# Reloads and the last matrix in quarter pieces: sixteen DMAs a chunk in place of four

## The chip, the cores and the metric

The kernel runs on one core of one Trainium2 chip, as one launch. The metric is the device time of that launch in microseconds (us). The engines are TensorE (PE), VectorE (DVE), ScalarE (ACT), GpSimd (POOL) and SyncE (SP). Each runs its own list of instructions in order; they meet only at semaphores. SyncE computes nothing here: it waits and issues DMAs, and 16 DMA engines carry out what SyncE, ScalarE and GpSimd issue.

## The reference

Two layers of a graph convolution on 6250 nodes and 200000 random edges, then a gather and a dense layer:

```python
def gcn_conv(x, W, b, src, dst, n):
    h = x @ W
    ...                                     # self loops, D^-1/2 (A+I) D^-1/2
    msgs = h[s] * norm[:, None]
    return jax.ops.segment_sum(msgs, d, num_segments=n) + b

g = jax.nn.relu(gcn_conv(service_emb, W1, b1, src, dst, 6250))
g = gcn_conv(g, W2, b2, src, dst, 6250)
ctx = g[context_idx].reshape(512, -1)                       # 3 x 32 features
x = jnp.concatenate([user_emb[user_idx], ctx], axis=1)      # 512 x 128
return x @ fc_W + fc_b                                      # 512 x 6250, float32
```

## The kernel before

**The adjacency as a matrix.** The kernel sorts the edges on VectorE (the first 310 us or so) and then builds the adjacency matrix in one-byte numbers from one-hot rows. Nodes lie in 49 blocks of 128. The matrix is built in chunks of destination blocks: `SIZES = [1, 2, 2] + [4] * 11`, that is `NG = 14` groups g. A group of 4 blocks has 196 tiles of 128 x 128 bytes, 25088 bytes in each of the 128 partitions. For each group, layer 1 is computed as soon as its tiles stand (`pair` and `aggregate` on TensorE, lines 1430 and 1448 into `psY`).

**Spill and reload.** SBUF holds three such groups in the slots of layer 1 (`SLOTS = 3`), and two more when the one-hot rows are no longer needed. The last three groups (11, 12, 13) stay; the other eleven are written to the DRAM tensor `adjacency_spill` (line 572) and read back for layer 2. `ORDER` is the order of layer 2: 11, 12, 13, 10, 9, ... 0. So places 3 to 10 of it are reloads of 4 blocks, 11 and 12 of 2 blocks, and 13 of 1 block. The prediction counts chunks by these places.

**Layer 2.** For place i, TensorE waits on `loaded` (line 1497) and on the PSUM tile of place i - 3, runs one matmul for each tile (`spread`, line 1448 into `pp`) and raises `y2_done`. VectorE reduces the tile (line 1220), finishes it (lines 1222 and 1212), and ScalarE's queue writes it to the DRAM table `context_table` (line 801), in rows of 128 bytes. SyncE runs ahead:

```python
sp.wait_ge(filled, pairs_before(NG))
for i in range(3, NG):
    if i >= 5:
        sp.wait_ge(y2_done, i - 4)
    part = -(-bytes_of(ORDER[i]) // LOAD_PARTS)
    for c in range(0, LOAD_PARTS * part, part):
        w = min(part, bytes_of(ORDER[i]) - c)
        sp.dma_start(...).then_inc(loaded[place2[i]], 16)        # line 597
for k in range(2):
    sp.wait_ge(y2_done, NG - 4 + k)
    load_fc(place2[(NG + k) % 5], k)
```

So the load for place i waits until place i - 5, whose slot it takes, is through; `load_fc` brings `fc_W` (k = 0, two DMAs a piece, since the rows of the user features are put behind the others, lines 584 and 585) and `fc_b` (k = 1, one row spread over all partitions, line 587). `fc_W` waits until place 9 is through, `fc_b` until place 10.

**The end.** GpSimd gathers three rows of the table for each of four batches (line 675), when the whole table is written. TensorE transposes the features (line 1529), multiplies them by W2 (line 1534), and then both TensorE (line 1538) and VectorE (line 1292) wait for all pieces of `fc_W` and `fc_b`. Then 4 x 13 matmuls in float32 (line 1549) are added to `fc_b` (line 1305) and written out by SyncE and ScalarE (line 522). Between layer 2 and the features TensorE runs 36 products of no use (`run_up`, line 1456).

Of the kernel before, what the change touches and what calls it, by code (L numbers as in the profile page):

```python
# [91 lines left out]
SPILL_PARTS = 4  # L92
RUN_UP = (8, 12, 36)
AHEAD_OF = {1: 12, 3: 6}
LOAD_PARTS = 4
FC_PART = 1568


UNIT = 2.0 ** -9
# [67 lines left out]
def bytes_of(g):  # L167
    return -(-tiles_of(g) // 2) * 2 * P
# [34 lines left out]
def gcn_kernel(nc, user_idx, context_idx, edge_index, user_emb, service_emb,  # L203
# [13 lines left out]
    with ctx:  # L217
# [309 lines left out]
        def _(sp):  # L527
# [50 lines left out]
            def load_fc(slot, what):  # L578
                tile = at(adj_at[slot], N * 4, F32)
                whole = fc_W if what == 0 else fc_b[None, :].to_broadcast((P, N))  # L580
                for c in range(0, N, FC_PART):
                    w = min(FC_PART, N - c)
                    if what == 0:
# [5 lines left out]
            with sp.If(is_bad == 0):  # L589
# [7 lines that stand above are left out]
# [220 lines left out]
        def _(dve):  # L817
# [468 lines left out]
            def mix_features(b):  # L1286

                dve.wait_ge(feat_mixed, b + 1)
                V.tensor_scalar(featT[0:CTX * D, b * P:(b + 1) * P], psX[0:CTX * D, b % 2 * P:(b % 2 + 1) * P], bias2[:, 0:1], None, ALU.add).then_inc(feat_ready, 1)  # L1289
            copy_features(0)  # L1290
            mix_features(0)
            dve.wait_ge(fc_in, 48 * -(-N // FC_PART))
            n = 0
# [15 lines left out]
        def _(pe):  # L1309
# [181 lines left out]
            with pe.If(is_bad == 0):  # L1491
                for i, g in enumerate(ORDER):
                    c = chunks_of(g)
                    tile = pp[i % 3]
                    if i >= 3:
                        pe.wait_ge(y2_read, i - 2)
                        pe.wait_ge(loaded[place2[i]], 16 * LOAD_PARTS * (i // 5 + (1 if i % 5 >= 3 else 0)))
                    for b in range(NH):
# [32 lines left out]
            def weigh_features(b):  # L1531

                pe.wait_ge(feat_copied, b + 1)
                MM(psX[0:CTX * D, b % 2 * P:(b % 2 + 1) * P], W2b[:], featT[0:CTX * D, b * P:(b + 1) * P], start=True, stop=True).then_inc(feat_mixed, 1)
            pe.wait_ge(users_in, 16 * BB)
            turn_features(0)
            weigh_features(0)
            pe.wait_ge(fc_in, 48 * -(-N // FC_PART))
            n = 0
# [33 lines left out]
```

## Time and profile before

| | us |
|---|---|
| three timed runs | 768.8, 770.29, 771.91 |
| their median | 770.29 |
| profiled execution | 772.33 |
| span of its instructions | 770.5 |
| TensorE busy | 587.4 (76%) |
| VectorE busy | 600.2 (78%) |
| ScalarE busy | 422.5 (55%) |
| GpSimd busy | 182.4 (24%) |
| TensorE's granted clock, mean | 0.92 of full speed |

All times are counted from the start of the span. "Busy" counts neither waits nor the issue of DMAs; the issues of SyncE's queue are rows of their own, marked SPq, whose length is the time that SyncE spent on them. "Issue" as the end of an idle time means that the engine waited for nothing that the profile shows. The share of the DMA engines is a mean over 16; it can come out a little over 1. The queues are q1 (SyncE), q10 (ScalarE), q0 (GpSimd), and q8 and q14, which carry instructions.

### The profile page before, as it was taken

How to read it: one execution, taken by the hardware profiler on the slowest of the kernel's cores; microseconds unless marked ns; L12 is line 12 of the kernel's file. 1: busy time of each engine (PE TensorE's matmuls, PEld its weight loads, DVE VectorE, ACT ScalarE, POOL GpSimd, SP SyncE). 2: the span in 40 equal slices, each digit the busy share in tenths (PEclk: the TensorE clock that was granted, in tenths of full speed). 3: DMA queues.
4: the chain of work that ended last, by engine and by line, in shares of the span. 5: the costliest groups of instructions: out<-in, count | busy, mean ns of one | idle time of the engine just before them, and what ended most of it. 6: DMA issues, size and time to landing. Idle time of an engine off the chain costs nothing.

```text
span 770.5 us, 21867 instructions
## 1 busy us (share of the span) xinstructions
PE 587.4 (76%) x9504; PEld 551.6 (72%) x9504; DVE 600.2 (78%) x1436; ACT 422.5 (55%) x770; POOL 182.4 (24%) x181
## 2 busy tenths in 40 slices
PE   0404662676929735478699999999999999997997
PEld 0304662675928725478699999999999998997643
DVE  9999999988999999787999999999984211111376
ACT  4993389797999111247588888888877000000000
POOL 1100000000000200377776666676200000000500
PEclk9999995978978965589899999999999999999999
DMA  7000000000000000235366665565200999859386
GB/s 127 2 0 1 1 1 1 1 2 1 2 3 2 5 0 1 58 92 173 100 211 209 209 209 205 183 204 199 66 3 3 359 414 408 289 153 303 86 316 284
DMA packets 39143, 94.13 MB, mean 122 GB/s; under 512 B 19097, under 2 KB 21843, under 8 KB 39044
## 3 DMA queue, kind: packets, MB, share of 16 engines
q1 hardware_dynamic: 24340, 74.28, 26.2%
q0 software_dynamic: 5216, 9.91, 6.1%
q10 hardware_dynamic: 9488, 8.52, 3.4%
q8 instruction: 76, 1.25, 0.7%
q14 instruction: 23, 0.19, 0.1%
HBM read 48.50 MB, written 44.18 MB: 120 GB/s over the span
## 4 chain that ended last, share of the span: by engine, by line
PE 55%; DVE 34%; issue 3%; ACT 3%; POOL 2%; DMA 1%; SPq 0%; DVEq 0%; POOLq 0%
PE pp L1430 17%; PE pp L1448 14%; PE psY L1448 13%; DVE arena L960 12%; DVE arena L961 11%; PE pp L1549 5%; PE psY L1346 3%; DVE arena L947 2%; POOL arena L655 2%; ACT arena L711 2%; PE pp L1366 1%; PE psX L1417 1%; DVE arena L958 1%; DVE arena L959 1%; DVE arena L955 1%
## 5 line engine op out<-in xcount | busy, mean ns | idle before, releaser
L1430 PE MATMUL pp<-arena 128*128 128x128 fp8e4 (+1 forms) x2401 | 189.4, 221 | 7.5 <-DVE arena L1140 6.3
L788 ACT ACTIVATE arena<-pp 128x512 uint16<-128x512 f32 x308 | 172.1, 584 | 42.0 <-PE pp L1430 39.7
L655 POOL DMA_INDIRECT arena<-ordered_keys,window x147 | 161.3, 1097 | 128.3 <-DMA ordered_keys<-arena 62.0
L711 ACT ACTIVATE arena<-arena,neg_word 128x780 fp8e4<-128x780 bf16 (+1 forms) x200 | 170.3, 942 | 10.4 <-PE psY L1346 10.4
L1430 PEld LDWEIGHTS pp<-arena 128*128 128x128 fp8e4 (+1 forms) x2401 | 148.4, 98 | 8.0 <-issue 6.0
L1448 PE MATMUL psY<-arena 128*128 128x96 bf16 x2401 | 150.5, 207 | 2.4 <-ACT y_s L772 2.1
L1448 PEld LDWEIGHTS psY<-arena 128*128 128x128 fp8e4 x2401 | 123.3, 98 | 2.9 <-ACT arena L788 2.6
L1139 DVE TENSOR_SCALAR arena<-arena 128x384 int32<-128x384 int32 (+5 forms) x224 | 110.8, 495 | 7.7 <-PE pp L1430 7.6
L1448 PE MATMUL pp<-arena 128*128 128x96 bf16 x2401 | 104.2, 206 | 9.0 <-issue 8.9
L1448 PEld LDWEIGHTS pp<-arena 128*128 128x128 fp8e4 x2401 | 102.7, 98 | 10.6 <-issue 10.5
L960 DVE TENSOR_TENSOR arena<-arena 128x832 f32<-128x832 f32 (+4 forms) x121 | 107.5, 889 | 3.1
L961 DVE TENSOR_TENSOR arena<-arena 128x832 f32<-128x832 f32 (+4 forms) x121 | 106.8, 883 | 0.0
L1366 PE MATMUL pp<-ident,arena 128*128 128x128 f32 x202 | 38.0, 361 | 77.1 <-DVE arena L961 75.8
L1346 PE MATMUL psY<-arena 128*128 128x128 fp8e4 x1024 | 69.2, 232 | 28.2 <-DVE arena L947 28.2
L1366 PEld LDWEIGHTS pp<-ident,arena 128*128 128x128 f32 x202 | 32.7, 189 | 80.3 <-DVE arena L961 78.5
L1346 PEld LDWEIGHTS psY<-arena 128*128 128x128 fp8e4 x1024 | 69.0, 141 | 29.1 <-issue 28.0
L1220 DVE TENSOR_REDUCE arena<-pp 128x128 f32<-128x384 f32 (+2 forms) x14 | 7.1, 507 | 94.4 <-PE pp L1448 94.4
L1140 DVE TENSOR_SCALAR arena<-arena 128x384 int32<-128x384 int32 (+5 forms) x224 | 72.7, 325 | 0.0
L764 ACT ACTIVATE arena<-arena,neg_low 128x128 f32<-128x128 f32 x147 | 47.9, 392 | 18.3 <-DMA arena<-ordered_keys,window 18.3
L640 POOL DMA_INDIRECT feat<-in_L_rec_user_emb_dram,ucl x4 | 4.6, 1146 | 218.1 <-DVEq L972 217.2
L675 POOL DMA_INDIRECT feat<-context_table,ccl x12 | 11.3, 945 | 173.5 <-DMA context_table<-arena 170.1
L1549 PE MATMUL pp<-arena 128*128 128x512 f32 (+1 forms) x104 | 43.1, 568 | 0.5 <-DVE arena L1289 0.5
(205 smaller groups left out, 543.6 us busy)
## 6 DMA issues: line engine op xcount, KB each, us to landing
arena<-adjacency_spill SPq DMA_DIRECT2D x32, 784.0 KB, 10.5
adjacency_spill<-arena SPq DMA_DIRECT2D x24, 768.0 KB
adjacency_spill<-arena SPq DMA_DIRECT2D x8, 832.0 KB
out_dram<-arena SPq DMA_DIRECT2D x12, 512.0 KB, 3.8
out_dram<-arena ACTq DMA_DIRECT2D x8, 512.0 KB, 3.8
arena<-adjacency_spill SPq DMA_DIRECT2D x8, 392.0 KB, 5.0
arena<-ordered_keys,window POOLq DMA_INDIRECT x147
arena<-in_L_rec_fc_b_dram SPq DMA_DIRECT2D x3, 784.0 KB, 12.1
```

The lines of the kernel that those rows point to most:

```text
L655: nc.gpsimd.indirect_dma_start(gath[:, k, q, :], None, ordered, bass.IndirectOffsetOnAxis(ap=window[:, q, d:d + 1], axis=0)).then_inc(gat[ ...
L711: ins = nc.scalar.activation(cols8[n % BUFS][:, 4 * u:4 * u + 4, 0:c1 - c0], high4[:, :, c0:c1], ACT.Sign, bias=neg_word[:, u:u + 1], satu ...
L788: nc.scalar.mul(adj16[g % SLOTS][:, m0 * P:m1 * P], bank(gp)[:, 0:(m1 - m0) * P], PAIR_SCALE).then_inc(evicted, 1)
L960: V.tensor_tensor(o_low, low, high, ALU.min)
L961: return V.tensor_tensor(o_high, low, high, ALU.max)
L1139: V.tensor_scalar(src32[h][:, i, :, 0:b - a], bit32[:, 0:4, a:b].bitcast(I32), abs(BIT - i), BITS, shift, ALU.bitwise_and)
L1140: ins = V.tensor_scalar(dst32[h][:, i, :, 0:b - a], bit32[:, 4:8, a:b].bitcast(I32), abs(BIT - i), BITS, shift, ALU.bitwise_and)
L1346: ins = MM(counts_of(s), cols8[n % BUFS][:, :, i], rows8[n % BUFS][:, :, i, :], start=False, stop=False)
L1366: ins = nc.tensor.transpose(ps[q][:, b * P:(b + 1) * P], src[:, c + b * P:c + (b + 1) * P], ident[:])
L1430: ins = MM(bank(gp)[:, (n - n0) // 2 * P:((n - n0) // 2 + 1) * P], src_hot(h, n - a), dst_hot(h, n - a), start=n % 2 == 0, stop=n % 2 == 1 ...
L1448: return MM(tile[:, dd * D3:(dd + 1) * D3], adj_tile(slot, n), features(layer, b), start=(n == 0), stop=(n == NH * c - 1))
L1549: MM(bank(n)[:, 0:w], featT[:, b * P:(b + 1) * P], fcW[:, c:c + w], start=True, stop=True).then_inc(fc_mm, 1)
```

## The change

Two constants change. Each reload is cut into sixteen pieces in place of four: 1568 bytes a partition where it was 6272 (for the groups of 2 blocks 784 where it was 3136, for the one of 1 block 400 where it was 1600). `fc_W` and `fc_b` go in pieces of 392 columns (1568 bytes) in place of 1568 columns. The counts in the waits follow. Nothing else changes; the lists of the other four engines are the same.

```diff
-LOAD_PARTS = 4
-FC_PART = 1568
+LOAD_PARTS = 16
+FC_PART = 392
```

SyncE's list before, from the branch behind the spills to the branch behind the loads of `fc_b` (`x32` stands for 32 of them in a row; `arena` is the SBUF area of all slots):

```order
L589 COMPARE_AND_BRANCH
L597 DMA arena<-adjacency_spill 128x6272 x32
L597 DMA arena<-adjacency_spill 128x3136 x8
L597 DMA arena<-adjacency_spill 128x1600 x4
L584 DMA arena<-in_L_rec_fc_W_dram 96x1568
L585 DMA arena<-in_L_rec_fc_W_dram 32x1568
```

Now the same place reads:

```order
L589 COMPARE_AND_BRANCH
L597 DMA arena<-adjacency_spill 128x1568 x128
L597 DMA arena<-adjacency_spill 128x784 x32
L597 DMA arena<-adjacency_spill 128x400 x16
L584 DMA arena<-in_L_rec_fc_W_dram 96x392
L585 DMA arena<-in_L_rec_fc_W_dram 32x392
```

There are 176 reloads where there were 44, and nothing has moved past them. Behind them, the pair of lines 584 and 585 came four times (the last with 1546 columns) and comes sixteen times (the last with 370). The end of the loads, in the list before:

```order
L584 DMA arena<-in_L_rec_fc_W_dram 96x1546
L585 DMA arena<-in_L_rec_fc_W_dram 32x1546
L587 DMA arena<-in_L_rec_fc_b_dram 128x1568 x3
L587 DMA arena<-in_L_rec_fc_b_dram 128x1546
L589 UNCONDITIONAL_BRANCH
```

and now:

```order
L584 DMA arena<-in_L_rec_fc_W_dram 96x370
L585 DMA arena<-in_L_rec_fc_W_dram 32x370
L587 DMA arena<-in_L_rec_fc_b_dram 128x392 x15
L587 DMA arena<-in_L_rec_fc_b_dram 128x370
L589 UNCONDITIONAL_BRANCH
```

The last piece of `fc_b`, for which the first matmul of line 1549 waits, is the 224th DMA of SyncE in this stretch; before it was the 56th.

## Rows read from the trace of the kernel before

**Rows 1.** The page: span, busy time by engine, chain by engine.

```profile
span 770.5 us, 21867 instructions
...
PE 587.4 (76%) x9504; PEld 551.6 (72%) x9504; DVE 600.2 (78%) x1436; ACT 422.5 (55%) x770; POOL 182.4 (24%) x181
...
PE 55%; DVE 34%; issue 3%; ACT 3%; POOL 2%; DMA 1%; SPq 0%; DVEq 0%; POOLq 0%
```

**Rows 2.** Groups by line, 598:714: count, busy, mean ns, idle before.

```profile
L1448 PE MATMUL pp<-arena 128*128 128x96 bf16 x2401 | 104.2, 206 | 9.0 <-issue 8.9
```

**Rows 3.** Timeline of TensorE: start, length, instructions, idle before.

```profile
612.86 5.60 PE L1448 MATMUL pp<-arena 128*128 128x96 bf16 x128 [0.23 <-issue]
...
672.91 27.55 PE L1448 MATMUL pp<-arena 128*128 128x96 bf16 x639 [0.82 <-issue]
701.81 5.57 PE L1448 MATMUL pp<-arena 128*128 128x96 bf16 x127 [1.35 <-issue]
710.02 2.67 PE L1448 MATMUL pp<-arena 128*128 128x96 bf16 x59 [2.63 <-issue]
```

**Rows 4.** DMA queues in 598:712, in 645.2:648, and in 626.5:628.5 (no instructions).

```profile
q8 instruction: 18, 0.29, 1.0%
...
q8 instruction: 1, 0.02, 2.1%
...
q1 hardware_dynamic: 146, 0.82, 97.5%
```

**Rows 5.** Timeline of VectorE: the reductions behind places 8 to 10.

```profile
681.40 0.56 DVE L1220 TENSOR_REDUCE arena<-pp 128x128 f32<-128x384 f32 x1 [8.34 <-PE pp L1448]
...
698.06 0.56 DVE L1220 TENSOR_REDUCE arena<-pp 128x128 f32<-128x384 f32 x1 [7.12 <-PE pp L1448]
```

**Rows 6.** The chain that ended last, 713 us on: start, length, what.

```profile
713.53 2.25 DMA context_table<-arena
...
723.22 7.11 PE pp L1549 x16
```

**Rows 7.** Timeline of SyncE's queue: start, length, DMAs issued.

```profile
598.29 4.13 SPq L597 DMA_DIRECT2D arena<-adjacency_spill  x8
...
626.59 1.74 SPq L597 DMA_DIRECT2D arena<-adjacency_spill  x4
...
645.26 2.62 SPq L597 DMA_DIRECT2D arena<-adjacency_spill  x4
...
663.45 2.37 SPq L597 DMA_DIRECT2D arena<-adjacency_spill  x4
...
690.04 1.58 SPq L585 DMA_DIRECT2D arena<-in_L_rec_fc_W_dram  x1
...
697.98 2.76 SPq L587 DMA_DIRECT2D arena<-in_L_rec_fc_b_dram  x4
...
L597 SPq DMA_DIRECT2D arena<-adjacency_spill x44: 319/432/1306, 598.3 to 682.6; - x44
```

**Rows 8.** DMA issues from 676 us: count, KB, median us from issue to landing.

```profile
arena<-adjacency_spill SPq DMA_DIRECT2D x4, 200.0 KB, 2.9
...
arena<-in_L_rec_fc_b_dram SPq DMA_DIRECT2D x1, 773.0 KB, 15.5
```

**Rows 9.** Queue q1 in 622:630, 672:678.5, 681.5:685.5; then engines in 683:683.5.

```profile
q1 hardware_dynamic: 574, 3.21, 96.6%
...
q1 hardware_dynamic: 578, 1.61, 71.5%
...
q1 hardware_dynamic: 539, 0.77, 65.1%
...
683.00:683.50 0.50, 0.50 (x16) 0.50 (x14) 0.00 (x0) 0.00 (x0) 0.00 (x0) 1.00 1.04 368
```

**Rows 10.** Stages by window (clock, DMA share, GB/s last); TensorE afterwards.

```profile
374.00:380.00 6.00, 3.65 (x39) 3.68 (x40) 5.86 (x19) 2.18 (x5) 4.59 (x5) 0.50 0.18 51
...
376.35 0.90 PE L1430 MATMUL pp<-arena 128*128 128x128 fp8e5 x7 [5.83 <-DVE arena L1140]
```

## The prediction

> **What bounds the kernel now.** I read the page first: the profiled span is 770.5 us (the execution itself 772.33 us; the median of the three timed runs is 770.29 us, so a difference in the span is carried over to the median as it is). No engine is full over the whole span and the chain is made mostly of TensorE and VectorE work [rows 1]. The change touches only DMAs that SyncE issues after the last aggregation of layer 1, so what counts is the stretch from 598 us to the end.
>
> In that stretch TensorE runs layer 2: fourteen chunks of matmuls of line 1448, each ended by the reduction of line 1220 on VectorE. The groups by line show 104.2 us of matmuls and 8.9 us in which TensorE stood still while it waited for nothing that the profile shows ("issue") [rows 2]. The timeline of TensorE shows their form: blocks of about 128 matmuls (5.60 us), and between them 0.2 to 0.8 us of idle time, then one of 1.35 and one of 2.63 us [rows 3]. From 672.91 us on, 639 matmuls run without a gap: there the DMA engines are no longer full. The gaps recur at a fixed number of instructions, and a 16 KB packet of the instruction queue is seen per block (18 from 598 to 712 us [rows 4]). I read them as fetches of TensorE's instructions that come late behind data packets. No wait on a reload shows anywhere: chunks without a gap follow each other at 8.33 us (from 681.40 to 698.06 us in two [rows 5]).
>
> Behind layer 2 the chain is: last reduction, the write of the table (2.25 us), three gathers on GpSimd, a transpose, and the first matmul of line 1549 at 723.22 us; from there TensorE sets the pace to the end, 16 matmuls in 7.11 us [rows 6]. That first matmul also waits for all pieces of fc_W and fc_b (lines 1538 and 1292). SyncE is done with issuing them at 700.7 us [rows 7], and the last lands 15.5 us after its issue [rows 8], by 716.2 us at the latest: 7 us ahead.
>
> **What the change does, part by part.** Bytes, waits and the work of the four compute engines stay; SyncE issues 176 reloads for 44 and 48 loads of fc_W and fc_b for 12, so 224 DMAs for 56.
>
> *Issuing.* Four DMAs in a row take 1.74 us, and the shortest, the first of a row, 0.32 us [rows 7]: the next ones come every (1.74 - 0.32) / 3 = 0.473 us. The row of all 44, those of 0.8 MB and the four of 0.2 MB, has a median of 0.432 us, hardly under that; so I price a quarter piece as a whole one, those of fc_W with 96 and 32 partitions too. 224 x 0.473 = 106.0 us. Four of the issues were far longer: rows of four took 2.62, 2.37 and 2.76 us instead of 1.74, and one DMA of fc_W 1.58 us instead of the median [rows 7]; that is 0.88, 0.63, 1.02 and 1.15 us too much, mean 0.92. An instruction packet starts while such a row is issued, as at 645 us, and none does in a row of 1.74 us, as at 626 us [rows 4]. With SyncE issuing all the time, each fetch would meet it: 17 fetches until TensorE is through x 0.92 = 15.6 us (below: 0; above: 0.071 us on each DMA besides, as the first eight took 4.13 us, (4.13 - 0.32) / 7 = 0.544 us, so 15.9 us more). SyncE's waits on y2_done don't bind: at 0.54 us a DMA a chunk costs it 8.7 us, no less than TensorE's 8.33, and it comes to fc_W at 598.3 + 176 x 0.54 = 693 us, where place 9 is through at 681.40 + 8.33 = 689.7 us. So the last piece is issued at 598.3 + 106.0 + 15.6 = 719.9 us and lands 2.9 us later, as the 200 KB reloads did [rows 8]: **722.8 us**.
>
> *Moving.* In full flow, 6272-byte rows made 3.21 MB in 8 us at 96.6% of the 16 engines: 415 GB/s at a full share. The 3136-byte rows come to 346, the 1600-byte rows, nearest to the new ones, to 296 (0.77 MB in 4 us at 65.1%) [rows 9]. But both are short bursts with their run-in; the best half microsecond of the 1600-byte rows is 368 GB/s at a share of 1.04, so 354. I take 354, since the new rows come in full flow; both ends are 296 and 415. A chunk of 3.21 MB then takes 9.1 us, eight of them 72.6 us; SyncE needs 128 x 0.473 = 60.5 us and 12 fetches, 11.0 us, to issue them, 71.5 us. The two are level, and the reloads are in time: the eighth lands at about 671 us plus a few, its matmuls start at 689.7 us, or 8.9 us earlier at most. That slack is the cover; it is gone only above 10.6 us a chunk (85 us over eight). The smaller chunks are bound by issue: 48 x 0.473 = 22.7 us.
>
> The Trainium skill, "DMA: Bandwidth & Descriptors", section "Bandwidth", says to batch to at least 1 MiB a DMA and that small ones are bound by descriptors; its fit, about 2.0 us plus the bytes at 436 GB/s, gives a 200 KB DMA 2.46 us by itself. Taken one after another, 224 of them would be 550 us by that estimate, and in the trace four such DMAs in flight had landed 2.9 us after their issue in the median [rows 8], with 0.43 us from one issue to the next; so they overlap and the fixed part is not added up. What is left of that rule is the slow rival below.
>
> *What comes back.* If short packets let the fetches through, TensorE's 8.9 us go. What speaks for it: no gap in the long stretch from 672.91 us, with small rows and engines that are often idle. Against: behind the first 3136-byte rows stood still a gap of 0.82 us [rows 3], and data in flight may count in bytes rather than in packets. Bounds: 0 and 8.9 us. I take nearly all, because SyncE then feeds the engines no faster than they drain, and no long queue stands. The first matmul of line 1549 starts 10.5 us after layer 2's last (710.02 + 2.67 us), so it could start at 714.3 instead of 723.2 us.
>
> The Trainium skill, "Runtime: NRT & Kernel Launch", section "Instruction fetch mechanics", says that the cost of crossing a 16 KiB block is mostly hidden. By it, these 8.9 us would not be fetches and would stay, and the sum would be that of the third rival. The trace has 16 KB packets at the pace of the blocks and a gap after most, which speaks against it here.
>
> *What is late next.* The first matmul then waits for the later of 714.3 us and fc (722.8 us): 723.1 us with the 0.3 us that the chain shows from a release to a start. Nothing is gained there: -0.1 us. TensorE's fill work and the first transpose would be through by some 714 us, and it stands still for some 9 us. Where it stood still for 5.83 us before 376.35 us, its clock was granted at 0.50, that is 1.2 GHz, from 374 to 380 us, so for 3.65 us at least after it set in again [rows 10]. Since TensorE sets the pace behind it, half of 3.65 us is lost: +1.8 us (bounds 0 and 3.6, if the clock doesn't fall or stays low for twice as long).
>
> **Sum.** -0.1 + 1.8 = +1.7 us on 770.3 us: **772.0 us**. Of the measurement: under 0.5% (3.9 us) can't be told from no change, so my forecast is no change.
>
> **The rivals.**
> *Fast: fetches don't hold SyncE up.* Then 106 us of issue end at 704.3 us and fc is in at 707.2 us, hidden again; the start is at 714.3 us and all 8.9 us are gained: 761.4 us. With fetches at 0.6 instead of 0.92 us fc lands at 717.4, the start is at 717.7, and it is 764.8 us, or 766.6 with the clock. It needs 0.51 us a DMA or less, (714.3 - 2.9 - 598.3) / 224. For: four cases are few, and the profile does not say why a fetch would hold SyncE up. Against: all four long issues have one.
> *Slow: the DMA engines need the full price of the 1600-byte rows.* At 296 GB/s eight chunks take 86.8 instead of 71.5 us, so fc lands 15.3 us later: 787 us; by 0.544 us an issue with the fetches on top it is the same size, 15.9 us. It decides from 0.544 us a DMA on ((720.3 - 598.3) / 224), where fc lands at 723.2 us; at 0.58 us it is +8 us. For: my central value stands right at that edge, and eight issues took 0.544 us without a fetch. Against: those came while the first rows still ran in.
> *Hidden: the gaps stay and fc is in time.* The fetch waits for bytes, not packets, layer 2 ends at 712.8 us as now, and fc lands at about 723 us: 770 to 771 us.
>
> **How the numbers follow.** Forecast 0.42 (own range 768 to 776), fast 0.22, slow 0.24, hidden 0.12. Faster by over 0.5% (below 766.4 us): the fast one and an edge of the forecast, 0.23. Slower (above 774.1 us): the slow one and a fifth of the forecast, 0.33. The rest, 0.44, within. The range leaves out the lower tip of the fast rival and the upper half of the slow one: 763 to 782 us.
>
> **What would show it.** Right: SyncE issues almost without a pause from 598 to about 720 us, the last fc_b piece at 718 to 722; gaps in line 1448 of under 2 us in sum; the last reduction at about 704; the first matmul of line 1549 at about 723 with fc as its releaser; a granted clock of 0.50 at its start. Wrong: issues at 0.48 us in spite of fetches (fast), reloads awaited in layer 2 or fc later than 728 us (slow), gaps as before (hidden).

## The result

| | before | changed |
|---|---|---|
| median of four timed runs | 771.1 us | 786.76 us |
| all of them | 768.8 to 773.83 | 783.47 to 787.66 |
| profiled execution | 772.33 us | 783.47 us |
| its span | 770.5 us | 781.6 us |

The ratio is 1.0164, 95% interval 1.0126 to 1.0202: the change makes the kernel slower, by 15.7 us in the medians and by 11.1 us between the two profiled executions. (The ratios here and below were recorded with the runs; they are not the quotients of the medians, which would be 1.0203 here.) The forecast of 772.0 us was wrong, and so was its range. Of the changed kernel the profiled execution is the fastest of the four; of the others there is no trace. So the text below explains 11.1 of the 15.7 us, and the other 4.6 us are not broken down.

### The profile page after: what moved, and what is told of

Same layout as the page of the kernel before. It is cut to its first block, busy times and chain, and to the rows that moved or that the text cites. A ratio compares the mean times of both kernels' runs of the same rounds, so it can differ in the third digit from the quotient of the medians.

```text
span 781.6 us, 22035 instructions
## 1 busy us (share of the span) xinstructions
PE 586.8 (75%) x9504; PEld 551.6 (71%) x9504; DVE 601.3 (77%) x1436; ACT 422.3 (54%) x770; POOL 182.6 (23%) x181
## 4 chain that ended last, share of the span: by engine, by line
PE 44%; DVE 33%; SPq 12%; ACT 3%; issue 3%; DMA 2%; POOL 2%; DVEq 0%; POOLq 0%
PE pp L1430 17%; PE psY L1448 13%; DVE arena L960 12%; DVE arena L961 11%; SPq L597 9%; PE pp L1549 6%; PE psY L1346 3%; PE pp L1448 3%; ACT arena L711 2%; POOL arena L655 2%; PE pp L1366 2%; DVE arena L947 2%; SPq L585 1%; SPq L584 1%; SPq L587 1%
## 5 line engine op out<-in xcount | busy, mean ns | idle before, releaser
L711 ACT ACTIVATE arena<-arena,neg_word 128x780 fp8e4<-128x780 bf16 (+1 forms) x200 | 170.3, 944 | 10.6 <-PE psY L1346 10.5
L1448 PE MATMUL pp<-arena 128*128 128x96 bf16 x2401 | 102.3, 206 | 0.3 <-issue 0.3
L1549 PE MATMUL pp<-arena 128*128 128x512 f32 (+1 forms) x104 | 44.7, 585 | 16.8 <-DMA arena<-in_L_rec_fc_b_dram 16.8
L1305 DVE TENSOR_TENSOR arena<-pp,arena 128x512 f32<-128x512 f32 (+1 forms) x52 | 33.9, 659 | 26.8 <-PE pp L1549 26.1
```

Source lines behind the costliest of these rows:

```text
L711: ins = nc.scalar.activation(cols8[n % BUFS][:, 4 * u:4 * u + 4, 0:c1 - c0], high4[:, :, c0:c1], ACT.Sign, bias=neg_word[:, u:u + 1], satu ...
L1448: return MM(tile[:, dd * D3:(dd + 1) * D3], adj_tile(slot, n), features(layer, b), start=(n == 0), stop=(n == NH * c - 1))
L1549: MM(bank(n)[:, 0:w], featT[:, b * P:(b + 1) * P], fcW[:, c:c + w], start=True, stop=True).then_inc(fc_mm, 1)
```

## The profile after

The page of the changed kernel: span, busy time, and the chain by engine and by line, against [rows 1].

```profile
span 781.6 us, 22035 instructions
...
PE 586.8 (75%) x9504; PEld 551.6 (71%) x9504; DVE 601.3 (77%) x1436; ACT 422.3 (54%) x770; POOL 182.6 (23%) x181
...
PE 44%; DVE 33%; SPq 12%; ACT 3%; issue 3%; DMA 2%; POOL 2%; DVEq 0%; POOLq 0%
PE pp L1430 17%; PE psY L1448 13%; DVE arena L960 12%; DVE arena L961 11%; SPq L597 9%; PE pp L1549 6%; PE psY L1346 3%; PE pp L1448 3%; ACT arena L711 2%; POOL arena L655 2%; PE pp L1366 2%; DVE arena L947 2%; SPq L585 1%; SPq L584 1%; SPq
```

The busy times are as before. But SyncE's queue (SPq), which had no share of the chain, has 12%: 9% at the reloads (line 597) and 3% at fc_W and fc_b. The timeline of TensorE (start, length, instructions, idle time before and its end) shows both halves of it:

```profile
600.24 102.25 PE L1448 MATMUL pp<-arena 128*128 128x96 bf16 x2401 [0.29 <-issue]
702.33 8.27 PE L1456 MATMUL pp<-above,ident 128*128 128x128 f32 x72
714.61 0.30 PE L1529 MATMUL psY<-ident,feat 128*128 128x128 f32 x1 [4.01 <-DMA feat<-context_table,ccl]
732.75 8.70 PE L1549 MATMUL pp<-arena 128*128 128x512 f32 x16 [16.84 <-DMA arena<-in_L_rec_fc_b_dram]
```

All 2401 matmuls of layer 2 run in one piece of 102.25 us, without one of the gaps of [rows 3]: layer 2 is over at 702.5 us where it was over at 712.7. Then TensorE is through with the features at about 716 us, and it stands still for 16.84 us, until fc_b is in. Its first matmul of line 1549 starts at 732.75 us, 9.5 us later than before, and sixteen take 8.70 instead of 7.11 us [rows 6]. These two, 9.5 and 1.6 us, are the 11.1 us.

SyncE's queue, with the issues merged; then three single issues on the chain; then the packets of instructions (count, MB, share) in 694:696, in 598:702.5 and in 598:727.6:

```profile
598.80 99.88 SPq L597 DMA_DIRECT2D arena<-adjacency_spill  x176
...
718.46 9.51 SPq L587 DMA_DIRECT2D arena<-in_L_rec_fc_b_dram  x16
...
694.23 0.44 SPq L597
...
694.71 1.58 SPq L597
...
696.34 0.43 SPq L597
...
q8 instruction: 1, 0.02, 3.9%
...
q8 instruction: 19, 0.31, 1.2%
...
q8 instruction: 21, 0.34, 1.1%
```

SyncE hardly waits (0.2 us in all): 176 reloads in 99.9 us, and the 224th DMA is issued at 727.5 us. A plain issue is 0.43 us and comes 0.474 us after the one before it. The one at 694.71 us, which takes 1.58 us, has a fetch of instructions beside it, a packet of 16 KB. 19 such fetches start before TensorE is through with layer 2, and 21 up to 727.6 us, where before it was 18 up to 712 [rows 4]. In the single rows of the trace each of the 21 has a long issue beside it, of 0.94 to 2.00 us; the time that these issues took beyond 0.43 us each is 19.9 us in sum, or 0.95 us a fetch.

Landing of the last piece (count, KB, us from issue to landing), and the engines while TensorE waits, with the granted clock, share of the DMA engines and GB/s as the last three numbers:

```profile
arena<-in_L_rec_fc_b_dram SPq DMA_DIRECT2D x1, 185.0 KB, 5.2
...
610.00:616.00 6.00, 6.00 (x146) 6.00 (x143) 0.00 (x0) 0.00 (x0) 0.00 (x0) 1.00 1.06 363
715.00:732.00 17.00, 0.62 (x2) 0.27 (x2) 0.59 (x2) 0.00 (x0) 5.70 (x7) 0.51 0.85 255
732.00:736.00 4.00, 3.25 (x4) 1.52 (x5) 0.69 (x1) 0.00 (x0) 0.00 (x0) 0.51 0.01 4
736.00:742.00 6.00, 6.00 (x16) 2.70 (x15) 4.66 (x7) 0.00 (x0) 0.00 (x0) 1.00 0.54 223
```

The last piece takes 5.2 us to land. In the reloads the rows of 1568 bytes go at 363 GB/s with a full share, where the 6272-byte rows had 415 [rows 9]. That is 13% less, but here SyncE's issuing sets the pace too; with more of the same rows queued (two issuers, below) it was 382. And the clock is at 1.2 GHz (0.51) from 715 to 736 us, back at 2.4 GHz from 736.

## Experiments

All start from the changed kernel unless said otherwise. Times of single executions vary in layer 1 already, so the table counts from the first matmul of layer 2. "Gaps": idle time within layer 2 that ends in "issue", from the waits. "Table": landing of the last write of context_table. "First": first matmul of line 1549. The ratio is that to the kernel before, timed on the same chip (its median there was 771.1 us for the changed kernel and 774.2 to 775.1 us for the others). "One run" means one execution, with no interval.

| kernel | layer 2 from | gaps | table | first | first, from layer 2 | span | ratio, 95% interval |
|---|---|---|---|---|---|---|---|
| before | 599.75 | 8.9 | 2.3 | 723.22 | 123.5 | 770.5 | |
| changed | 600.24 | 0.3 | 3.8 | 732.75 | 132.5 | 781.6 | 1.0164 (1.0126 to 1.0202) |
| quarter reloads only | 599.98 | 0.3 | 9.5 | 726.84 | 126.9 | 776.8 | 1.0072 (1.0042 to 1.0103) |
| quarter fc only | 601.47 | 4.8 | 5.2 | 725.64 | 124.2 | 775.1 | 1.0022 (0.9995 to 1.0049) |
| halves | 601.20 | 6.3 | 3.6 | 724.62 | 123.4 | 773.3 | 1.0027 (1.0003 to 1.0052) |
| two issuers | 600.42 | 5.5 | 3.6 | 725.48 | 125.1 | 774.7 | 1.0051 (1.0024 to 1.0077) |
| half the products | 599.68 | 0.3 | 3.2 | 724.39 | 124.7 | 773.6 | one run |
| long run-up | 601.86 | 0.3 | 3.6 | 736.09 | 134.2 | 785.7 | one run |
| paced, 3 x 392 KB | 600.21 | 0.3 | 3.5 | 751.07 | 150.9 | 801.4 | 1.0316 (1.0271 to 1.036) |
| paced, 2 x 784 KB | 598.96 | 1.2 | 2.3 | 738.52 | 139.6 | 787.5 | 1.0201 (1.0164 to 1.0238) |
| paced, 3 and 3 | 601.76 | 6.5 | 2.2 | 722.24 | 120.5 | 769.5 | 1.0032 (1.0008 to 1.0056) |
| paced, 3 and 2 | 601.78 | 4.2 | 5.5 | 723.28 | 121.5 | 772.6 | 0.9995 (0.9971 to 1.0018) |
| paced, 2 and fc free | 600.08 | 3.1 | 13.0 | 728.39 | 128.3 | 777.7 | 1.0064 (1.0025 to 1.0104) |
| quarter reloads, no fc | 603.06 | 0.3 | 2.2 | 719.06 | 116.0 | 766.4 | 0.9867 (0.9826 to 0.9909) |

### One part of the change alone

Quarter reloads only:

```diff
-FC_PART = 392
+FC_PART = 1568
```

> Only the reloads are in sixteen pieces; fc_W and fc_b are in four again. Theory A (SyncE's issuing is the bound: 0.474 us a DMA and about 1 us more for each instruction fetch of TensorE): the 176 reloads end at about 699 us as in the changed kernel (698.7), the 12 loads of fc are issued by 706 us and are then bound by the DMA engines, as in the kernel before (about 20 us for 6.4 MB), in by 718 to 720 us; first matmul of line 1549 at about 719 us, span 767 to 770 us, that is 0 to 4 us below the kernel before. Theory B (the DMA engines' price of short rows in the reloads is what made it slower): the span stays within 4 us of the changed kernel's 781.6 us. Both expect no gaps in line 1448.

Quarter pieces of fc_W and fc_b only:

```diff
-LOAD_PARTS = 16
+LOAD_PARTS = 4
```

> Only fc_W and fc_b are in quarter pieces; the reloads are in four again. Theory A: SyncE comes to fc_W as early as before (about 690 us), issues 48 DMAs in 48 x 0.474 + 4 fetches = 27 us, the last at about 717 us, landed by 722; the gaps in the reload part of line 1448 are back (about 4.6 us of 8.9), those behind it smaller. First matmul of line 1549 at about 722 us, span 768 to 771 us. Theory B': the pieces of fc themselves cost the time (their landing, 5 us, and their short rows), so the span stays above 776 us.

Each part alone costs less than half of the whole: 1.0072 and 1.0022 against 1.0164, and the latter can't be told from no change. That points at the number of DMAs in the one stretch: 224 here, 188 and 92 there. But the spans, 776.8 and 775.1 us, are above what theory A gave, 767 to 770 and 768 to 771 us. The chain of the kernel with quarter reloads only, from the end of layer 2 on, shows something that was in neither theory; the last row is the landing of the last piece of fc_b:

```profile
699.05 3.18 DMA arena<-adjacency_spill
...
705.45 9.53 DMA context_table<-arena
...
718.19 6.41 DMA feat<-context_table,ccl
...
726.84 8.47 PE pp L1549 x13
...
arena<-in_L_rec_fc_b_dram SPq DMA_DIRECT2D x1, 773.0 KB, 19.3
```

Layer 2 waits 2.3 us for the last reload, and then the last write of the table, 16 KB, takes 9.53 us where it took 2.25 [rows 6], and the third gather 6.41 us. fc_W and fc_b were issued behind the reloads, at 699 to 706 us, and their traffic runs beside these small DMAs. With quarter pieces of fc only, the write took 5.20 us. Two things limit this reading. The last piece of fc_b was issued at 706.1 us and landed 19.3 us later, at 725.4 us; so even with a quick write and quick gathers the first matmul would have come 1.4 us sooner at most. What cost this kernel its time is again SyncE's list, which comes to fc_W at 699.5 us where it was 689.7 before. And after the long idle time sixteen matmuls took 9.76 us instead of 7.11, which is 2.7 us more of the span.

### Halves

```diff
-LOAD_PARTS = 16
-FC_PART = 392
+LOAD_PARTS = 8
+FC_PART = 784
```

> Half pieces everywhere: 88 reloads of 3136 bytes a partition and 24 loads of fc. Theory A: SyncE needs 112 x 0.474 = 53 us of issue and about 8 us of fetches, is never the bound and waits for y2_done again; fc is in before 712 us. If the gaps of line 1448 go with the length of a row, span about 762 us (8.9 us below the kernel before); if they go by the depth of the queue in bytes, which SyncE fills again here, they stay at 4 to 9 us and the span is 766 to 771 us. Theory B (engines' price of shorter rows): between the kernels before and changed, 773 us or more.

The gaps are back (6.3 us), though the rows are half as long as before. SyncE issues faster than the engines move here, and the queue is deep: the reloads between 612 and 662 us take 9.8 us to land in the median, as the 10.0 us before, against 4.1 in the changed kernel. This is the second form of the expectation, with the span 2 us above it. The span alone, 773.3 us, would also fit theory B; but nothing waited for a reload or for fc, and counted from layer 2 the first matmul is where it was before (123.4 and 123.5 us). The 2.6 us of gaps that went came back in a write of 3.56 us and a third gather of 3.92 us. That gather was issued at 718.9 us, when the traffic of fc was over (a share of 0.14 in 717:719), and why it was slow stays open.

### Two queues issue the reloads

```diff
-                    for c in range(0, LOAD_PARTS * part, part):
+                    for c in range(0, LOAD_PARTS * part, 2 * part):
...
+            def load_odd(i):
+                part = -(-bytes_of(ORDER[i]) // LOAD_PARTS)
+                for c in range(part, LOAD_PARTS * part, 2 * part):
+                    w = min(part, bytes_of(ORDER[i]) - c)
+                    act.dma_start(at(adj_at[place2[i]] + c, w, U8), spill[ORDER[i], :, c:c + w]).then_inc(loaded[place2[i]], 16)
...
                 for i, g in enumerate(ORDER):
                     write_table(i, g)
+                    if i + 5 < NG:
+                        act.wait_ge(y2_done, i + 1)
+                        load_odd(i + 5)
```

ScalarE waits for the spills and for `filled` as SyncE does, and issues its half of places 3 and 4 first.

> The changed kernel with the same 176 quarter reloads, but every second one is issued by ScalarE's queue, which is idle there but for the table; bytes, rows and pieces are those of the changed kernel. Theory A: SyncE has 88 reloads in place of 176, comes to fc_W when place 9 is through (about 684 us), issues the 48 pieces in 27 us, the last by 711 us, landed by 716; first matmul of line 1549 at about 716 us, span 763 to 766 us. Theory B (the DMA engines are the bound, they show a share of 1.05 through the reloads): fc lands within 4 us of the changed kernel's 732.7 us, span 778 us or more. It also shows whether the gaps of line 1448 come back when the queue is deep with short rows.

Bytes, pieces and rows are those of the changed kernel, and the first matmul comes at 725.48 us, 7.4 us sooner counted from layer 2. So the number of DMAs that one queue has to issue is what bound it, and not the price of the rows. The hoped-for 716 us were not reached: fc_b was in at 725.4 us, and the gaps of TensorE came back. Its timeline, and the engines in the same stretch:

```profile
643.86 5.60 PE L1462 MATMUL pp<-arena 128*128 128x96 bf16 x128 [0.61 <-issue]
...
616.00:628.00 12.00, 11.06 (x258) 10.84 (x255) 1.94 (x5) 0.00 (x0) 0.00 (x0) 1.00 1.07 382
```

The DMA engines are as full as in the changed kernel (1.07 and 1.06 in this window) and no slower (382 and 376 GB/s), and the rows are as short. What differs is how much is queued: landing takes 7.2 and 8.4 us in the two queues against 4.1. So short rows alone don't let a fetch through. Whether it is the depth or the second queue, this run can't tell; the paced kernels below have one queue.

### Half the products of layer 2

```diff
-                    for b in range(NH):
+                    for b in range(0, NH, 2):
```

> The changed kernel, in which TensorE leaves out every second block of products of layer 2 (so its output is not the reference's); SyncE's list is untouched. TensorE then fetches instructions about half as often in layer 2. Theory A (each fetch holds SyncE's issuing by about 1 us): some 9 of the 21 delays are gone, the last piece of fc_b is issued about 9 us sooner, at 717 to 720 us instead of 727.5, and the first matmul of line 1549 starts at 722 to 726 us. Theory C (the long issues are back-pressure of the DMA engines, and only fall together with the fetches): the bytes and rows are the same, so the last issue stays at 727 us, within 2 us.

TensorE leaves out 24 of 49 source blocks in layer 2, and fetches 12 blocks of instructions in the stretch instead of 21. SyncE's list is the same. Its end, the first matmul behind fc_b, and the count of fetches:

```profile
708.72 10.34 SPq L587 DMA_DIRECT2D arena<-in_L_rec_fc_b_dram  x16
...
724.39 9.05 PE L1549 MATMUL pp<-arena 128*128 128x512 f32 x16 [15.06 <-DMA arena<-in_L_rec_fc_b_dram]
...
q8 instruction: 12, 0.20, 0.6%
```

From the first reload (598.22 us) to the end of the list are 120.8 us instead of 129.2 (598.80 to 727.97): 8.4 us less for 9 fetches less, or 0.93 us a fetch. This is theory A's number, and it speaks against the long issues being mere back-pressure of the DMA engines: bytes, rows and list are the same. It is one execution; the 21 pairs of a fetch and a long issue in the changed kernel give nearly the same number, 0.95 us. As TensorE is twice as quick, it waits for reloads nine times, 32.4 us in sum; it changes nothing in SyncE's pace.

### A longer run-up

```diff
-RUN_UP = (8, 12, 36)
+RUN_UP = (8, 12, 110)
```

> The changed kernel with 110 instead of 36 fill products behind layer 2, so that TensorE works on until about 728 us, close to where fc is in. Expected: granted clock 1.00 at the first matmuls of line 1549, sixteen of them in about 7.1 us as before in place of 8.70; the fill adds at least one fetch of instructions, so fc may be about 1 us later. Net -1.5 to 0 us against the changed kernel's 781.6 us. If the clock is not what made the 16 matmuls slower, they still take 8.7 us.

```profile
730.00:736.00 6.00, 1.89 (x14) 1.32 (x12) 0.64 (x2) 0.00 (x0) 0.00 (x0) 0.82 0.67 242
736.00:740.00 4.00, 3.91 (x5) 1.83 (x6) 0.78 (x2) 0.00 (x0) 0.00 (x0) 0.50 0.00 0
...
736.09 9.41 PE L1549 MATMUL pp<-arena 128*128 128x512 f32 x16 [3.03 <-DMA arena<-in_L_rec_fc_b_dram]
```

It missed: the span is 785.7 us, 4.1 us above the changed kernel's, where -1.5 to 0 was expected, and the clock was low. Layer 2 began 1.6 us later, and counted from there fc came 1.7 us later. It was in at 736 us, TensorE was idle for most of 731 to 736 us, and the clock was at 0.50 from 736 to 740 us. Sixteen matmuls took 9.41 us, 2.3 us more than at full clock. The fill had kept TensorE busy to 731.1 us, but the 3.03 us of waiting for fc_b and the short products ahead of it were followed by the low clock all the same. So this run does not show what a pause-free start would give.

### Pacing

Starting from the pieces of the kernel before or from halves, SyncE waits until an earlier piece has landed before it issues the next. Each piece in flight has a semaphore of its own:

```diff
+IN_FLIGHT, FC_IN_FLIGHT = 3, 2
...
-        loaded = [sem(f"loaded{k}") for k in range(5)]
+        loaded = [[sem(f"loaded{k}_{j}") for j in range(IN_FLIGHT)] for k in range(5)]
...
+                        landed = loaded[place2[i]][k % IN_FLIGHT]
+                        if k >= IN_FLIGHT:
+                            sp.wait_ge(landed, 16 * (before * len(range(k % IN_FLIGHT, LOAD_PARTS, IN_FLIGHT)) + k // IN_FLIGHT))
```

> Half pieces (8 a chunk, 784 columns of fc), and SyncE issues a reload only when the third before it has landed, a piece of fc when the second before it has. So at most about 1.2 MB are queued on the DMA engines (2.9 us at 415 GB/s). If TensorE's gaps and the late table writes and gathers both come from the depth of the queue: no or few gaps in line 1448 (below 3 us), layer 2 over at 703 to 706 us, the first transpose about 9 us behind it, fc in before it, span 762 to 765 us, below both kernels. If the gaps don't depend on the queue's depth, 4 to 9 us of them stay and the span is 767 us or more. A reload that comes late would show as a wait on adjacency_spill.

> The pieces of the kernel before (4 a chunk, 1568 columns), with at most two reloads and one piece of fc in flight, so up to 1.6 MB queued (3.9 us). It holds the size of the pieces still and changes only the depth of the queue. By depth: gaps in line 1448 get smaller but not all vanish (2 to 5 us of 8.9), and the table and gathers behind layer 2 are faster than in the kernel before; span 763 to 768 us. If rows of 6272 bytes are what delays a fetch, the gaps stay near 8.9 us and the span at 770 us.

The first row is from the kernel with 3 x 392 KB, the others are from the one with 2 x 784 KB:

```profile
696.18 18.18 PE L1464 MATMUL pp<-arena 128*128 128x96 bf16 x392 [4.80 <-DMA arena<-adjacency_spill]
...
623.75 72.50 PE L1464 MATMUL pp<-arena 128*128 128x96 bf16 x1699 [0.27 <-issue]
...
738.52 8.79 PE L1567 MATMUL pp<-arena 128*128 128x512 f32 x16 [21.71 <-DMA arena<-in_L_rec_fc_b_dram]
...
698.29 5.98 DMA arena<-in_L_rec_fc_W_dram
...
704.64 5.18 DMA arena<-in_L_rec_fc_W_dram
```

With rows of 6272 bytes, as before, and two reloads in flight, the gaps fall from 8.9 to 1.2 us: 1699 matmuls in a row. Of the 8.9 us, 4.0 stood behind the long pieces of fc (the last two of [rows 3]), so the fair comparison, in the reloads alone, is 5.0 with 1.2 us. It shows that long rows let the fetches through when little is queued. But both kernels are slower, and both expectations missed (762 to 765 and 763 to 768 us). Three pieces of 392 KB can't feed layer 2 (it waits 13.1 us for reloads in five places), and with one piece of fc in flight one lands every 4 to 6 us, so TensorE waits 21.7 us for fc_b.

The next two loosen it, both with the pieces of the kernel before; the third frees fc altogether.

> The pieces of the kernel before, with at most three reloads (2.4 MB, 5.7 us) and three pieces of fc in flight. Two reloads in flight took TensorE's gaps away but loaded too slowly, and one piece of fc in flight took 4 to 6 us each. Depth theory: gaps between those of the kernel before and of two in flight, 2 to 5 us; fc in before the features; span 763 to 768 us. If three in flight are as good as no pacing (the queue is deep enough again to hold a fetch up by its full 2 to 3 us), the gaps are 8 to 9 us and the span is that of the kernel before.

> As the run with three and three, but with two pieces of fc in flight. fc_W and fc_b are 8 pieces; with two in flight one lands about every 2.9 us, 23 us in all from about 687 us: in by 710 to 714 us, just ahead of the features. The table's last write and the gathers stand behind less traffic (2 to 3 us and about 3 us). Span 762 to 768 us. If fc is late instead, the first matmul of line 1549 waits for it and the span is 770 us or more.

> Two reloads in flight, fc not paced (its 12 DMAs in a row). Layer 2 is over at about 703 us as with two in flight before, fc_W starts at about 698 us and the 6.4 MB take some 20 us: in at 718 to 720 us. Depth theory for the tail: the table's last write and the gathers stand behind this traffic as in the run with quarter reloads alone (9.5 and 6.4 us), so the first matmul of line 1549 is at 720 to 725 us and the span at 768 to 774 us. If the tail is not delayed, the first matmul is at about 719 us and the span at 766 us.

The first three rows are from three and two in flight, the last two from two in flight with fc free:

```profile
706.22 2.88 PE L1464 MATMUL pp<-arena 128*128 128x96 bf16 x64 [1.43 <-issue]
...
723.28 9.11 PE L1567 MATMUL pp<-arena 128*128 128x512 f32 x16 [0.53 <-DVE arena L1304]
...
709.94 5.50 DMA context_table<-arena
...
707.23 12.98 DMA context_table<-arena
...
728.39 9.13 PE pp L1567 x16
```

All three spans, 769.5, 772.6 and 777.7 us, lie above what was expected (768, 768 and 774 us at the most). Counted from layer 2, the first matmul comes 3.0 us sooner with three and three and 2.0 us sooner with three and two than in the kernel before, in the profiled executions; timed, they are 1.0032 and 0.9995, so no gain. (The profiled execution with three and three is the fastest of its twelve.) With three and two the 2.0 us are lost again at once: TensorE had stood still for 3.97 us for a gather, and sixteen matmuls took 9.11 us in place of 7.11.

Part of what layer 2 gains comes back in the table's last write. Layer 2 ended at 709.1 us with three and two and at 706.4 us with fc free, where it was 712.7, and the writes took 5.50 and 12.98 us. In the kernel before this write landed at 715.8 us; with halves at 715.7 and with three and two at 715.4, each 0.7 to 1.5 us after the traffic of fc had ended. That is no rule: with quarter reloads only it landed at 715.0 us and the traffic of fc went on to 725, and with one piece of fc in flight the write took 2.3 us in the middle of it.

In the reloads alone the gaps fall with the time that a reload took to land (its median in 612:662): 5.0 us of gaps at 10.0 us before, 4.7 at 9.8 with halves, 2.8 at 8.9 with three and three, 2.2 at 8.8 with three and two, 3.1 at 7.0 with two and fc free, 1.2 at 6.3 with 2 x 784 KB, 0.3 at 4.1 in the changed kernel. The reloads are paced alike in the two kernels with two in flight, so 1.2 and 3.1 us show how much one execution can differ. Two issuers, with 5.5 us of gaps at 7.2 and 8.4 us, don't fit into this row.

### The same without fc

From the kernel with quarter reloads only; nobody loads fc_W and fc_b or waits for them:

```diff
-                for c in range(0, N, FC_PART):
+                for c in range(0, 0, FC_PART):
...
-            dve.wait_ge(fc_in, 48 * -(-N // FC_PART))
-            pe.wait_ge(fc_in, 48 * -(-N // FC_PART))
```

> The kernel with quarter reloads alone, with the loads of fc_W and fc_b left out and nobody waiting for them (so the last stage works on stale numbers and the output is not the reference's). In the kernel with quarter reloads alone, TensorE had no gaps and was through at 704.6 us, yet the first matmul of line 1549 started at 726.8, since the table's last write took 9.5 us and the gathers 6.4 us. Theory (the 6.4 MB of fc stand ahead of these small DMAs on the DMA engines, and this is where TensorE's gain goes): table's last write about 2.3 us, gathers about 2.4 us, first matmul of line 1549 at 713 to 716 us, span 762 us or a little less. If the two are slow for another reason (GpSimd's own issue, or the end of the reloads), the first matmul stays at 720 us or later.

```profile
709.51 2.19 DMA context_table<-arena
...
714.91 2.41 DMA feat<-context_table,ccl
...
719.06 7.13 PE L1547 MATMUL pp<-arena 128*128 128x512 f32 x16 [0.44 <-DVE arena L1289]
```

Without the traffic of fc the write takes 2.19 us instead of 9.53 and the gather 2.41 instead of 6.41; so there it was this traffic that made them slow. From layer 2 to the first matmul are 116.0 us instead of 126.9; but this run takes away the wait for fc_b as well, which would have held most of these 10.9 us, as said above. The first matmul came later than the expected 713 to 716 us, since this execution entered layer 2 at 603.06 us, 3 us late, and waited 3.2 us for the last reload; the span was 766.4 us, where 762 or a little less was expected.

## Why the prediction was wrong

**What was right.** The order of events was the predicted one: SyncE issues almost without a pause, each fetch of instructions holds it up, layer 2 runs without gaps and ends ten microseconds sooner, and then TensorE waits for fc_b with its clock down. A plain issue came every 0.474 us (predicted 0.473) and the reloads were in time. So the mechanism held, and what failed were sizes in the sum. The clock cost 1.6 us (predicted 1.8): 8.70 against 7.11 us for sixteen matmuls.

**The step that failed** is the sum under *Issuing*, "the last piece is issued at 719.9 us and lands 2.9 us later: 722.8 us". Measured were 727.5 us, 5.2 us, 732.7 us. In parts:

- The fetches were put at 17 x 0.92 = 15.6 us, counted "until TensorE is through". 19 started in layer 2 and two more behind it, while SyncE was still issuing: 21, at 0.95 us each 19.9 us. That is 4.3 us more, 3.7 of them by the count.
- From 598.80 us to the 224th issue at 727.53 us are 128.7 us, of which 223 x 0.474 = 105.7 us are plain issue; 23.0 us remain. Without the 19.9 us of the fetches that leaves 3.1 us, for which the sum had no term. 1.9 us of them are among the sixteen pieces of fc_b, which took 9.51 us in place of 16 x 0.474 = 7.6 with no 16 KB fetch beside them; why they did is open.
- 4.3 and 3.1 us, less 0.3 us (the sum took 224 steps for 223) and with a start 0.5 us later, are the 7.6 us by which the last issue was late.
- The landing was put at 2.9 us after the 200 KB reloads. It was 5.2 us for the last piece of fc_b, and 4.9 us in the median of the fifteen before it: 2.3 us more.
- Together 9.9 us. The forecast had 0.544 us a DMA as the point from which the change loses; it was 128.7 / 223 = 0.577 us. The prediction itself said that its central value was right at that edge, and that at 0.58 us it would be +8 us; the range should have reached further up.

**The features** were put at 714.3 us; they were ready at about 716.4 us, though layer 2 was over 10.2 us sooner than before, because the write and the gathers ran in the middle of fc's traffic. Here it cost nothing, since fc was later still. In the kernels where fc was in by about 715 us (halves, three and two) the slower write and gathers, and the clock behind them, took the gain away. The step "could start at 714.3 instead of 723.2 us" took the 10.5 us behind layer 2 as a constant; here they were some 14 us.

**The rivals.** The slow one has the right sign and nearly the size (787 us), but its mechanism is not the cause: the short rows moved at 363 GB/s and not at 296, no reload was late, and with two issuers the same rows were through 7.4 us sooner. Its second form, a higher price of each issue (0.577 us over the whole list), is what happened, through more fetches. The fast rival is refuted: of the 21 fetches none was free. The hidden one held that a fetch waits for bytes and not for packets; two issuers, halves, and two in flight fit that, but in the changed kernel SyncE kept the queue shallow, and so the gaps went.

**The rules of the Trainium skill.** The one of "Runtime: NRT & Kernel Launch", section "Instruction fetch mechanics", that crossing a block of instructions is mostly hidden, agrees with the traces for TensorE where little is queued (0.3 us of gaps in the changed kernel) and not behind a deep queue (8.9 us before), and the 0.95 us that a fetch cost SyncE in the changed kernel were not hidden. The advice of "DMA: Bandwidth & Descriptors", section "Bandwidth", to batch DMAs, points the right way here, but the price was that of the issue and not that of the transfer. The fit that the prediction quotes from that page was measured on DMAs that GpSimd issued, and these are SyncE's; no term of the sum used it.

**Not settled:** why a fetch by TensorE holds up an issue by SyncE; the runs show that it does, and for how long. Why the pieces of fc_b took 5 us to land and some of their issues 0.7 to 1.0 us. And the 4.6 us between the profiled execution and the median of the changed kernel.

## What to carry to other kernels

Count the DMAs of a queue and multiply: here 0.474 us each, plus nearly 1 us for each fetch of another engine's instructions, against the time that the queue has; cutting pieces is free only up to there. A queue kept shallow lets small and urgent transfers through (instructions, a last table write, a gather), and one that is merely filled ahead delays them. And before a stall is counted as a gain, ask what the engine meets when it is through sooner: here layer 2 was over 10.2 us sooner, and TensorE waited 16.84 us for the last matrix.

## What the runs showed of the hardware

- An issue on SyncE's queue that meets a fetch of TensorE's instructions took 0.94 to 2.00 us in place of 0.43 (21 of 21 fetches in the changed kernel); nine fetches fewer made the same list 8.4 us shorter.
- Gaps of TensorE at its fetches, in the reloads alone, fell with what was queued: on one queue from 5.0 us at a median landing of 10.0 us to 1.2 and 3.1 us at 6.3 and 7.0 us (all with 6272-byte rows), and to 0.3 us at 4.1 us (1568). Half the row length with the queue as deep left 4.7 us. Two queues with 1568-byte rows had 5.5 us.
- With the DMA engines full (612 to 662 us), rows of 6272 bytes moved 410 GB/s, rows of 3136 bytes 405, and rows of 1568 bytes 366 from one queue and 382 from two.
- A 16 KB write took 2.2 us with nothing beside it, 2.3 us beside one piece of fc in flight, and 9.5 and 13.0 us when nearly all of the 6.4 MB had been issued ahead of it on another queue.
